# Six gather buffers and six one-hot buffers, in two steps of three groups, in the graph convolutions of a three-layer graph network

## The chip, the cores and the metric

The kernel runs on one core of one Trainium2 chip. The metric is the device time of one execution in microseconds (us). The engines are TensorE (PE for matmuls, PEld for loading weights), VectorE (DVE), ScalarE (ACT), GpSimd (POOL) and the synchronising engine SyncE (SP). SP, ACT and POOL also issue transfers; their queues are written SPq, ACTq and POOLq.

## What is computed

12500 nodes with 96 features, 400000 edges sorted by destination. A first layer passes messages with edge attributes; it is not touched here. Two graph convolutions follow, and with them this change:

```python
def _gcn_conv(x, edge_index, edge_weight, W, b):
    h = x @ W
    row = concatenate([edge_index[0], loop]); col = concatenate([edge_index[1], loop])
    w = concatenate([edge_weight, ones])
    deg = segment_sum(w, col); dinv = where(deg > 0, rsqrt(deg), 0)
    norm = dinv[row] * w * dinv[col]
    return segment_sum(norm[:, None] * h[row], col) + b
for W, b, Wr, br in layers:            # two layers
    h_in = x
    xc = _gcn_conv(x, edge_index, edge_weight, W, b)
    g = sigmoid(h_in @ Wr + br)
    x = relu((1.0 - g) * h_in + g * xc)
```

## The kernel before

After the edge layer, two convolution layers run (l = 0, 1), each over all edges in one pass. In each, the edges go two ways.

The 1736 "main" tiles of 128 edges make 217 groups of 8 tiles. For a group, POOL issues 8 indirect transfers (line 927), each gathering 128 rows of the scaled node table, into one of three row buffers `conv_g[b]`, b = g mod 3; VectorE writes weighted one-hot matrices of the destinations inside a window of 64 nodes into one of two buffers `conv_s[h]`, h = g mod 2, with two operations (`spread_group`, lines 1826 and 1830); TensorE multiplies the 8 tiles into one PSUM bank `sg[h]` (`segment`, line 1123, 16 matmul records for 8 matmuls in float32); VectorE adds the 64 columns to the accumulator `acc` at a start that it reads from a table (`add_group`, line 1841).

The 1400 "side" tiles go through dense adjacency blocks written by the edge layer. 35 units of 40 tiles are each 14 pieces; ACT loads a piece of 980 KB into one of seven ring slots (`load_piece`, line 1352) once the piece seven earlier has been eaten; TensorE multiplies its 7 blocks (`piece`, line 1137, 14 records); after the 14th piece ACT copies the sums to `side_out` (line 1368) and VectorE adds 40 short column ranges to `acc` (`add_side`, line 1854), in four parts of ten.

The two ways are interleaved by hand. TensorE first does the lead, 7 groups, and then per unit 14 pieces with a segment after pieces 1, 3, 6, 8, 10 and 13 (`SEGMENT_AFTER`), 6 groups a unit. In the first 28 units, "mix" work for one half chunk of nodes is done too: TensorE's gate product (line 1145) after the first segment and its own product (line 1149) after the third, VectorE's seven operations (lines 1861 to 1876) after the fourth side part. SP loads the two inputs of that mix (lines 736 and 737) and stores its results (lines 740 and 741).

What orders the work are counting semaphores: `seg` (segments done), `acc` (sums added), `weighted` (one-hots ready), `eaten` (pieces), `out` (side sums copied), `added` (side ranges added). Before the change:

- POOL gathers group n once `seg` shows group n-3; the ids come in steps of three groups, loaded by SP (`load_step`, three transfers, two buffers) once `seg` shows the last group of two steps earlier.
- VectorE spreads group n once `seg` shows n-2, then waits for segment n-1 and adds it, then does a side part.
- TensorE's segment n waits for its rows, for `weighted` of n and for `acc` of n-2.
- SP's order in a unit: wait for the mix of the unit before, load the mix inputs; wait for `seg`, load a step; wait for `added`, load the bases of the side ranges; wait for the mix, store it; wait for the unit's last `seg`, load a step.

## Time and profile before

| | us |
|---|---|
| median of 3 runs | 11193.3 |
| lowest, highest | 11172.85, 11203.12 |
| the profiled execution's own time | 11224.96 |
| its span from first to last instruction | 11223.1 |
| mean granted TensorE clock | 0.85 of 2.4 GHz |

The convolutions take the second half: the first gather of layer 0 is issued at 5693.7 us, layer 0's last piece ends at 8354 us, layer 1 gathers from 8460.5 us and ends its pieces at 11133 us. In a row of the page, "idle before" is the time the engine sat idle just before such instructions, and the name behind the arrow is what ended most of it. "issue" means that no releaser shows; "remote" means that a semaphore update from elsewhere ended the wait. A mean of line 1137 or 1123 counts overlapping halves of one float32 matmul, so the spacing of the starts, not the mean, is the pace.

### The profile page before, as it was taken

Reading aid. Unit: us, or ns where it says so; the run is one execution under the profiler, and the core shown is the slowest. Engines: PE = TensorE matmul, PEld = TensorE weight load, DVE = VectorE, ACT = ScalarE, POOL = GpSimd, SP = SyncE. Lnnn points to the kernel's source line nnn. Section 1 sums busy time; section 2 is a strip of 40 time slices with the busy share of each in tenths; the row PEclk is TensorE's granted clock in tenths of the full one; section 3 lists DMA queues with packets and bytes.
Section 4 is the critical chain, followed back from the end, with each engine's and each line's share of the span. In section 5 each row is a group of like instructions: output and inputs, shape, how many; then the busy total and the mean of one; then the engine's idle time right before and its main releaser. Section 6 shows DMA issues by size and latency. Waiting matters only on the chain. (4 is left out here: it accounts for less than half of the span.)

```text
span 11223.1 us, 161106 instructions
## 1 busy us (share of the span) xinstructions
PE 8285.4 (74%) x40104; PEld 5619.5 (50%) x40104; DVE 5185.2 (46%) x17514; ACT 2896.1 (26%) x6502; POOL 6745.8 (60%) x6696
## 2 busy tenths in 40 slices
PE   5567667676666667766758888888876888888886
PEld 4334444444444444444445655556554555555554
DVE  5566666666666666666622222222222222222223
ACT  4345555555555555555400000000000000000000
POOL 4665555565655565666456666666655666666663
PEclk7688888888888888888768998888887888888887
DMA  4345555565655566666447767677665676766666
GB/s 152 81 130 169 169 170 168 171 174 168 173 167 172 168 173 171 171 172 173 136 147 234 239 228 233 228 235 240 222 201 181 229 235 228 236 233 228 233 225 200
DMA packets 1329031, 2149.86 MB, mean 192 GB/s; under 512 B 306427, under 2 KB 1079948, under 8 KB 1328700
## 3 DMA queue, kind: packets, MB, share of 16 engines
q10 hardware_dynamic: 142400, 986.64, 24.7%
q1 hardware_dynamic: 925996, 684.95, 20.8%
q0 software_dynamic: 260560, 477.49, 15.9%
q14 instruction: 55, 0.45, 0.0%
q8 instruction: 20, 0.33, 0.0%
HBM read 1587.45 MB, written 560.99 MB: 191 GB/s over the span
## 5 line engine op out<-in xcount | busy, mean ns | idle before, releaser
L927 POOL DMA_INDIRECT hid<-conv_table,hid x3452 | 3389.3, 982 | 1962.6 <-issue 1031.5
L883 POOL DMA_INDIRECT hid<-src_table,src_ids x3127 | 3174.7, 1015 | 2115.5 <-ACT msg L1255 1127.1
L1137 PE MATMUL bd<-ring,table_sb 128*96 128x280 f32 x13720 | 3618.3, 421 | 307.3 <-issue 245.0
L1137 PEld LDWEIGHTS bd<-ring,table_sb 128*96 128x96 f32 x13720 | 2341.8, 173 | 1501.4 <-issue 647.2
L1033 PE MATMUL bd<-one_hot_dst,one_hot_src 128*128 128x343 bf16 x8400 | 1753.8, 353 | 1463.7 <-ACT blocks L1263 1193.1
L1033 PEld LDWEIGHTS bd<-one_hot_dst,one_hot_src 128*128 128x128 bf16 x8400 | 840.9, 108 | 2270.9 <-issue 1811.0
L1263 ACT ACTIVATE blocks<-bd 128x686 f32<-128x686 f32 x1400 | 1116.9, 798 | 2289.4 <-remote 1503.7
L1841 DVE TENSOR_TENSOR acc<-acc,sg 96x64 f32 x434 | 94.7, 218 | 2956.3 <-remote 1568.4
L1123 PE MATMUL sg<-conv_hot,hid 128*96 128x64 f32 x6944 | 774.9, 258 | 618.4 <-issue 466.1
L1123 PEld LDWEIGHTS sg<-conv_hot,hid 128*96 128x96 f32 x6944 | 746.1, 176 | 707.7 <-issue 622.5
L1368 ACT ACTIVATE side_out<-bd,side_flag 96x280 f32<-96x280 f32 x70 | 34.3, 490 | 4015.9 <-PE bd L1137 2436.3
L1255 ACT ACTIVATE msg<-hid,msg 128x96 f32<-128x96 f32 x3136 | 905.4, 362 | 153.7 <-DVE msg L1565 124.5
L1052 PEld LDWEIGHTS sg<-hot,msg 128*98 128x98 f32 x6272 | 780.3, 200 | 328.1 <-issue 154.8
L1052 PE MATMUL sg<-hot,msg 128*98 128x64 f32 x6272 | 818.5, 284 | 158.7 <-ACT msg L1255 129.5
L1854 DVE TENSOR_TENSOR acc<-acc,side_out 96x7 f32 x2800 | 462.5, 165 | 947.8 <-issue 620.2
L1585 DVE TENSOR_SCALAR one_hot_src<-one_hot_src,side_now 128x128 bf16<-128x128 bf16 x4200 | 809.4, 259 | 0.0
L1022 PE MATMUL pa<-w_attr,attr 128*128 128x384 f32 x1568 | 677.1, 561 | 62.1 <-DMA attr<-in_attr 36.0
L1022 PE MATMUL pb<-w_attr,attr 128*128 128x384 f32 x1568 | 674.0, 558 | 47.8 <-issue 36.0
L1565 DVE TENSOR_SCALAR msg<-gate_t 128x4 f32<-128x4 f32 x784 | 152.0, 194 | 1196.5 <-ACT gate_t L1248 1008.2
L1242 ACT ACTIVATE hid<-hid 128x768 f32<-128x768 f32 x784 | 654.1, 834 | 195.5 <-issue 104.7
L1582 DVE TENSOR_SCALAR one_hot_dst<-iota_z,side_now 128x688 bf16<-128x688 f16 x1400 | 563.5, 402 | 0.0
L1541 DVE TENSOR_TENSOR hid<-pb,hid 128x768 f32<-128x768 f32 x392 | 373.4, 952 | 293.6 <-DMA hid<-src_table,src_ids 209.6
(208 smaller groups left out, 5412.3 us busy)
## 6 DMA issues: line engine op xcount, KB each, us to landing
ring<-adjacency ACTq DMA_DIRECT2D x980, 980.0 KB
adjacency<-blocks SPq DMA_DIRECT2D x700, 686.0 KB
hid<-conv_table,hid POOLq DMA_INDIRECT x3452
attr<-in_attr SPq DMA_DIRECT2D x392, 128.0 KB
hid<-src_table,src_ids POOLq DMA_INDIRECT x3127
conv_table<-table_sb SPq DMA_DIRECT2D x28, 336.0 KB, 4.7
feat_half<-feat_keep SPq DMA_DIRECT2D x56, 168.0 KB
buf_h<-dinv_rows SPq DMA_DIRECT2D x56, 168.0 KB
```

The costliest lines, as they stand in the source:

```text
L883: pool.indirect_dma_start(out=hid[s][:, t, :], out_offset=None, in_=src_rows, in_offset=bass.IndirectOffsetOnAxis(ap=src_ids[s // 2][:, j: ...
L927: pool.indirect_dma_start(out=conv_g[b][:, t, :], out_offset=None, in_=conv_rows[l], in_offset=bass.IndirectOffsetOnAxis(ap=conv_ids[j][:, ...
L1022: last = nc.tensor.matmul(attr_ps[s % 2][:, 512 * h:512 * h + 2 * H2], attr[s // 2][:, P * (s % 2):P * (s % 2 + 1)], w_attr[:, 2 * H2 * h: ...
L1033: op = nc.tensor.matmul(bd[:, 512 * h:512 * h + HALF_Z], y[:, 1 + k, :], z[:, Z_PAD * h:Z_PAD * h + HALF_Z], start=(k == 0), stop=(k == 2))
L1052: op = nc.tensor.matmul(sg[s // 2][0:ACC_ROWS, 0:WINDOW], msg[s % 2][:, t, :], hot[s % 2][:, t, :], start=(s % 2 == 0 and t == 0), stop=(s ...
L1123: op = nc.tensor.matmul(sg[h][0:D, 0:WINDOW], conv_g[b][:, t, :], conv_s[h][:, t, :], start=(t == 0), stop=(t == GROUP - 1))
L1137: op = nc.tensor.matmul(side_ps, table_sb[:, D * k:D * (k + 1)], ring[slot][:, :, QUAD_FANS * b:QUAD_FANS * (b + 1)], start=(k == 0), stop ...
L1242: nc.scalar.activation(flat, flat, ACT.Gelu).then_inc(s_gelu, 1)
L1255: op = nc.scalar.activation(m[:, t, 0:D], hid[s][:, t, 0:D], ACT.Copy, scale=m[:, t, GATE_ROW:GATE_ROW + 1])
L1263: nc.scalar.activation(blocks[h][:, :, FAN * t4:FAN * (t4 + 1)].rearrange("p (h b) d -> p h b d", h=2), bd[:, :].rearrange("p (h z) -> p h ...
L1582: v.tensor_scalar(z[:, :], iota_z[:, :], side_now[:, 4, t:t + 1], None, ALU.is_equal)
L1585: op = v.tensor_scalar(y[:, 1 + k, :], y[:, 0, :], side_now[:, 1 + k, t:t + 1], None, ALU.mult)
```

## The change

Per layer, rows and one-hots get six buffers each, as two steps j = 0, 1 of three slots. The added buffers lie in space that is free in this phase (the tiles that hold `feat_in`, `x_c`, `buf_h`, `buf_b` at other times, and one new tile). POOL gathers group n once `seg` shows n-6. The three sums of a step are columns of one PSUM bank `sg[j]`; VectorE adds them once all three segments of the step are done, and TensorE's first segment of a step waits until the sums of two steps before have been added. VectorE spreads a whole step ahead of the additions, and does side parts behind the second and third slot of each step, the mix at the end of the unit. SP loads ids for step k+2 once the rows of step k have landed, and the other two streams once the one-hots of step k are weighted, both in the first part of the unit; it no longer waits for `seg` at the unit's end, so that the load of the mix inputs stands right behind the store of the mix before. The core of the diff:

```diff
-CONV_SPARED = [min(GROUP - 1, max(0, PAD_TILES - GROUP * b)) for b in range(STEP_GROUPS)]
-SEG_CREDIT, ACC_CREDIT, SIDE_CREDIT = 3, 2, 1
+CONV_SPARED = [min(GROUP - 1, max(0, PAD_TILES - GROUP * b)) for b in range(LEAD_GROUPS)]
+SEG_CREDIT, ACC_CREDIT, SIDE_CREDIT = 2 * STEP_GROUPS, STEP_GROUPS, 1
...
+        rows_of = [[feat_space[0][:, 0:GROUP * D], feat_space[1][:, 0:GROUP * D], rows_own[0]],
+                   [rows_own[1], rows_own[2], rows_more[:, :]]]
+        hots_of = [[hot_own[0][:, :], x_c[0][:, 0:GROUP * WINDOW], x_c[1][:, 0:GROUP * WINDOW]],
+                   [hot_own[1][:, :], buf_h[1][:, 0:GROUP * WINDOW], buf_b[1][:, 0:GROUP * WINDOW]]]
...
-                def load_step(j, k, late, s=cv[l], skip=0):
-                    g = k * STEP_GROUPS - LEAD_SKIP + skip
-                    groups, width = STEP_GROUPS - skip, GROUP * (STEP_GROUPS - skip)
+                def load_ids(j, k, late, skip=0):
                     sp.dma_start(conv_ids[j][:, GROUP * skip:].rearrange("p (g t) -> p g t", t=GROUP),
-                                 io["src"][bass.ds(late * LATE_GROUPS + g, groups), :, :].rearrange("g p t -> p g t")
-                                 ).then_inc(s[f"step{j}"], 16)
+                                 io["src"][bass.ds(late * LATE_GROUPS + group_of(k, skip), STEP_GROUPS - skip), :, :
+                                           ].rearrange("g p t -> p g t")).then_inc(s_conv_ids[j], 16)
+
+                def load_edges(j, k, late, skip=0):
+                    tile0, width = GROUP * group_of(k, skip), GROUP * (STEP_GROUPS - skip)
                     sp.dma_start(conv_rel[j][:, GROUP * skip:],
-                                 rel_keep[:, bass.ds(late * MAIN_TILES + g * GROUP, width)]).then_inc(s[f"step{j}"], 16)
+                                 rel_keep[:, bass.ds(late * MAIN_TILES + tile0, width)]).then_inc(s_conv_edges[j], 16)
                     sp.dma_start(conv_wt[j][:, GROUP * skip:],
-                                 io["weight"][:, bass.ds(late * SIDE_TILES + g * GROUP, width)]).then_inc(s[f"step{j}"], 16)
+                                 io["weight"][:, bass.ds(late * SIDE_TILES + tile0, width)]).then_inc(s_conv_edges[j], 16)
+
+                def load_step_after(j, m, k, n0, late, s=cv[l]):
+
+                    for slot in slots_of(k):
+                        wait_apart(sp, s_rows[j][slot], rows_gathered(m, j, slot))
+                    load_ids(j, k + 2, late)
+                    wait_apart(sp, s["weighted"], n0 + group_of(k, STEP_GROUPS))
+                    load_edges(j, k + 2, late)
...
                     if more:
-                        wait_apart(sp, s["seg"], n0 + u * UNIT_GROUPS + (LEAD_GROUPS + STEP_GROUPS + SEG_CREDIT))
-                        load_step(1, u * 2 + 5, late)
+                        for k in (LEAD_STEPS, LEAD_STEPS + 1):
+                            load_step_after(k % 2, u + k // 2, u * 2 + k, n0, late)
                     wait_apart(sp, s["added"], nu * SIDE + SIDE_CREDIT)
                     load_base(u)
                     if mix:
                         wait_apart(sp, m["done"], h0 + u + 2)
                         store_mix_half(u)
-                    if more:
-                        wait_apart(sp, s["seg"], n0 + u * UNIT_GROUPS + (LEAD_GROUPS + UNIT_GROUPS + SEG_CREDIT))
-                        load_step(0, u * 2 + 6, late)
 
...
-                def gather_group(g, n, slot, j, b, spared, s=cv[l], l=l):
-                    wait_apart(pool, s["seg"], n + (SEG_CREDIT - STEP_GROUPS + 1))
+                def gather_group(n, j, slot, spared, s=cv[l], l=l):
+                    wait_apart(pool, s["seg"], n + (SEG_CREDIT - 2 * STEP_GROUPS + 1))
...
+                def gather_step(k, j, m, n0, c0):
+
+                    wait_apart(pool, s_conv_ids[j], c0 * (16 * STEPS_OF[j]) + m * 16 + 16)
+                    for slot in slots_of(k):
+                        g = group_of(k, slot)
+                        gather_group(n0 + g, j, slot, CONV_SPARED[g] if isinstance(g, int) else 0)
+
+                def conv_unit(u, n0, c0):
+                    for k in (LEAD_STEPS, LEAD_STEPS + 1):
+                        gather_step(u * 2 + k, k % 2, u + k // 2, n0, c0)
 
...
-                def segment(g, n, b, h, j, s=cv[l]):
-                    pe.wait_ge(s[f"gath{b}"], gathered_group(j, b))
-                    pe.wait_ge(s["weighted"], n + 1)
-                    pe.wait_ge(s["acc"], n + (ACC_CREDIT - 1))
+                def segment(k, j, m, slot, n0, s=cv[l]):
+                    if slot == 0 and not (isinstance(k, int) and k < 2):
+                        pe.wait_ge(s["acc"], n0 + group_of(k - 1, ACC_CREDIT))
+                    pe.wait_ge(s_rows[j][slot], rows_gathered(m, j, slot))
+                    pe.wait_ge(s["weighted"], n0 + group_of(k, slot + 1))
                     for t in range(GROUP):
-                        op = nc.tensor.matmul(sg[h][0:D, 0:WINDOW], conv_g[b][:, t, :], conv_s[h][:, t, :],
-                                              start=(t == 0), stop=(t == GROUP - 1))
+                        op = nc.tensor.matmul(sg[j][0:D, WINDOW * slot:WINDOW * (slot + 1)], conv_g[j][slot][:, t, :],
+                                              conv_s[j][slot][:, t, :], start=(t == 0), stop=(t == GROUP - 1))
                     op.then_inc(s["seg"], 1)
 
...
-                def spread_group(g, n, h, j, slot, s=cv[l]):
-
-                    dve.wait_ge(s["seg"], n + (SEG_CREDIT - 1))
+                def spread_group(n, j, slot, s=cv[l]):
+
+                    dve.wait_ge(s["seg"], n + (SEG_CREDIT - 2 * STEP_GROUPS + 1))
                     cols = slice(GROUP * slot, GROUP * (slot + 1))
...
+                def spread_step(k, j, m, slot, n0, c0):
+
+                    if slot == slots_of(k)[0]:
+                        dve.wait_ge(s_conv_edges[j], c0 * (32 * STEPS_OF[j]) + m * 32 + 32)
+                    spread_group(n0 + group_of(k, slot), j, slot)
+
+                def add_group(k, j, slot, n0, late, sides, s=cv[l]):
+
+                    g = group_of(k, slot)
                     start = dve.value_load(base_i[0:1, bass.ds(late * LATE_GROUPS + g, 1)], min_val=0, max_val=NODES)
                     window = acc[0:D, bass.ds(start, WINDOW)]
-                    dve.wait_ge(s["acc"], n + ACC_CREDIT)
+                    dve.wait_ge(s["acc"], n0 + g + ACC_CREDIT)
                     dve.wait_ge(s["added"], sides + SIDE_CREDIT)
-                    dve.wait_ge(s["seg"], n + (1 + SEG_CREDIT))
-                    v.tensor_tensor(window, window, sg[h][0:D, 0:WINDOW], ALU.add).then_inc(s["acc"], 1)
+                    dve.wait_ge(s["seg"], n0 + group_of(k, STEP_GROUPS) + SEG_CREDIT)
+                    v.tensor_tensor(window, window, sg[j][0:D, WINDOW * slot:WINDOW * (slot + 1)],
+                                    ALU.add).then_inc(s["acc"], 1)
 
...
-                def conv_unit(u, n0, u0, h0, k0, late, with_sides, with_mix, s=cv[l]):
+                def conv_unit(u, n0, u0, h0, c0, late, with_sides, with_mix, more):
 
...
-                        spread_group(g0 + at, m0 + at, at % 2, j, slot)
-                        done = ADD_PART * min(ADD_PARTS, max(0, i - 1)) if with_sides else 0
-                        add_group(g0 + (at - 1), m0 + (at - 1), (at - 1) % 2, late, n + (done - past))
-                        if with_sides and 1 <= i <= ADD_PARTS:
-                            add_side(done, done + ADD_PART, nu - 1, m0 + at)
-                        if i == ADD_PARTS and with_mix:
-                            mix(u, h0 + u)
+                    done, past = 0, SIDE if with_sides else 0
+                    for k in (LEAD_STEPS, LEAD_STEPS + 1):
+                        for slot in range(STEP_GROUPS):
+                            if more or k == LEAD_STEPS:
+                                spread_step(u * 2 + (k + 1), (k + 1) % 2, u + (k + 1) // 2, slot, n0, c0)
+                            add_group(u * 2 + (k - 1), (k - 1) % 2, slot, n0, late, n + (done - past))
+                            if with_sides and slot > 0:
+                                add_side(done, done + ADD_PART, nu - 1, n0 + group_of(u * 2 + (k - 1), slot + 1))
...
-                    conv_unit(0, n0, u0, h0, k0, late, False, True)
+                    for k in range(-1, LEAD_STEPS):
+                        for slot in slots_of(k + 1):
+                            spread_step(k + 1, (k + 1) % 2, (k + 1) // 2, slot, n0, c0)
...
-                        conv_unit(u, n0, u0, h0, k0, late, True, True)
-                    with dve.Fori(HALVES, UNITS) as u:
-                        conv_unit(u, n0, u0, h0, k0, late, True, False)
-                    add_group(MAIN_GROUPS - 1, n0 + (MAIN_GROUPS - 1), (MAIN_GROUPS - 1) % 2, late, all0 + (UNITS - 1) * SIDE)
+                        conv_unit(u, n0, u0, h0, c0, late, True, True, True)
+                    with dve.Fori(HALVES, UNITS - 1) as u:
+                        conv_unit(u, n0, u0, h0, c0, late, True, False, True)
+                    conv_unit(UNITS - 1, n0, u0, h0, c0, late, True, False, False)
+                    for slot in range(STEP_GROUPS):
+                        add_group(STEPS - 1, (STEPS - 1) % 2, slot, n0, late, all0 + (UNITS - 1) * SIDE)
```

## Rows read from the trace of the kernel before

**Rows 1.** page of the profile, parts 1 and 5: busy us, share, count; the gathers.

```profile
PE 8285.4 (74%) x40104; PEld 5619.5 (50%) x40104; DVE 5185.2 (46%) x17514; ACT 2896.1 (26%) x6502; POOL 6745.8 (60%) x6696
...
L927 POOL DMA_INDIRECT hid<-conv_table,hid x3452 | 3389.3, 982 | 1962.6 <-issue 1031.5
```

**Rows 2.** windows: length, busy us (records) of PE, PEld, DVE, ACT, POOL; clock, DMA.

```profile
5926.00:7845.00 1919.00, 1616.99 (x7693) 1138.99 (x7692) 517.13 (x1690) 29.02 (x52) 1231.32 (x1251) 0.89 0.70 233
7845.00:8354.00 509.00, 421.91 (x2040) 299.44 (x2040) 109.68 (x404) 3.43 (x7) 313.96 (x323) 0.89 0.64 216
8694.00:10621.00 1927.00, 1632.57 (x7698) 1135.92 (x7696) 519.62 (x1690) 29.14 (x52) 1234.33 (x1253) 0.89 0.70 232
10621.00:11134.00 513.00, 424.25 (x2040) 303.38 (x2041) 109.62 (x404) 3.43 (x7) 309.77 (x320) 0.88 0.63 212
```

**Rows 3.** timeline of PE: start us, duration, line, operation, count, idle before it.

```profile
7667.39 1.49 PE L1123 MATMUL sg<-conv_hot,hid 128*96 128x64 f32 x16
7675.35 1.24 PE L1123 MATMUL sg<-conv_hot,hid 128*96 128x64 f32 x13
7677.63 0.27 PE L1123 MATMUL sg<-conv_hot,hid 128*96 128x64 f32 x1 [1.04 <-issue]
...
7687.50 7.83 PE L1137 MATMUL bd<-ring,table_sb 128*96 128x280 f32 x22 [0.80 <-issue]
```

**Rows 4.** timeline of POOL beside Rows 3; 14 more gathers in the gap.

```profile
7666.15 0.95 POOL L927 DMA_INDIRECT hid<-conv_table,hid  x1 [2.01 <-remote]
...
7686.15 0.95 POOL L927 DMA_INDIRECT hid<-conv_table,hid  x1 [0.30 <-issue]
7690.04 0.95 POOL L927 DMA_INDIRECT hid<-conv_table,hid  x1 [2.94 <-remote]
```

**Rows 5.** windows of line 1137 alone: no gathers beside it, then with gathers.

```profile
8337.00:8354.00 17.00, 15.83 (x68) 10.62 (x66) 1.00 0.02 4
...
7754.00:7771.00 17.00, 11.26 (x42) 6.60 (x42) 0.88 0.51 158
```

**Rows 6.** timelines of PE, DVE and POOL at the start of layer 0.

```profile
5739.01 2.79 PE L1123 MATMUL sg<-conv_hot,hid 128*96 128x64 f32 x16 [7.59 <-DMA hid<-conv_table,hid]
5754.18 2.82 PE L1123 MATMUL sg<-conv_hot,hid 128*96 128x64 f32 x16 [12.38 <-DVE conv_hot L1830]
...
5777.32 0.22 PE L1123 MATMUL sg<-conv_hot,hid 128*96 128x64 f32 x1 [1.30 <-issue]
...
5798.32 0.59 PE L1123 MATMUL sg<-conv_hot,hid 128*96 128x64 f32 x3 [1.13 <-issue]
...
5752.58 0.22 DVE L1841 TENSOR_TENSOR acc<-acc,sg 96x64 f32 x1 [23.64 <-remote]
...
5753.25 0.97 POOL L927 DMA_INDIRECT hid<-conv_table,hid  x1 [5.98 <-remote]
```

**Rows 7.** timeline around the gate product of one unit (SPq: transfers issued by SP).

```profile
7704.24 0.09 SPq L736 DMA_DIRECT2D feat_half<-feat_keep  x1
...
7711.15 0.99 PE L1145 MATMUL bd<-feat_half,conv_w 96*96 96x448 f32 x2 [2.31 <-DMA buf_h<-dinv_rows]
```

**Rows 8.** waits: who for whom, total us, times, longest; PEld by layer, then POOL.

```profile
PEld bd L1145 <- issue: 35.9, 15, 6.4
...
PEld bd L1145 <- issue: 33.3, 15, 6.9
...
POOL hid L927 <- PE sg L1123: 461.6, 138, 7.1
POOL hid L927 <- remote: 433.3, 183, 6.1
```

**Rows 9.** timeline at the end of layer 0: last sum, then the side columns.

```profile
8355.73 0.22 DVE L1841 TENSOR_TENSOR acc<-acc,sg 96x64 f32 x1 [10.76 <-PE sg L1123]
...
8357.44 2.81 DVE L1854 TENSOR_TENSOR acc<-acc,side_out 96x7 f32 x10 [1.50 <-issue]
...
8375.58 1.09 DVE L1939 TENSOR_TENSOR t_c<-acc,buf_h 96x896 f32<-96x896 f32 x1
```

110 lines of the change are left out of this document (49 added, 61 removed).

## The prediction, made before the changed kernel was run

> **What bounds the kernel now.** Read the windows of the convolution first [rows 2]. The ScalarE counts give the units: a mix unit has two ScalarE records (52 are 26 units), a later one has one. So a mix unit takes 1919/26 = 73.8 us and 1927/26 = 74.1 us in layers 0 and 1, a unit without mix 509/7 = 72.7 and 513/7 = 73.3. No engine is full: PE's busy share there is 84% and its clock 0.89.
>
> Then read what TensorE's instructions cost undisturbed. From one segment to the next, over a segment and two pieces, 7.96 us pass (7667.39 to 7675.35) [rows 3]. A unit is six segments and 14 pieces; two pieces are that less the segment's share, which I put at 1.3 (an estimate), so 6.6 us, so a unit is 7 x 6.6 + 6 x 1.3 = 54 us, plus 2 for the mix products. 16 to 18 us of each unit are lost.
>
> The timelines of TensorE and GpSimd beside each other show where. From 7666.15 POOL runs 16 gathers, two groups, without a rest (start to start 1.25 to 1.6 us) [rows 4]. Ten microseconds into that run TensorE falls from a record every 0.1 us to one every 1.4 to 2.1, inside a segment, where nothing is waited for, and stays so to 7687.50, just as the run ends [rows 3]. The first 17 us after a layer's gathers are done have 68 records of line 1137 at clock 1.00; 17 us inside a unit with gathers have 42 [rows 5]. At the layer's start it is grosser: a segment under way at 5777.3 creeps to 5798.3 [rows 6]. Semaphore updates suffer as well: a segment issued from 5739.01 to 5741.8 is added by VectorE only at 5752.58, and POOL, idle for 5.98 us, resumes at 5753.25, on the same update [rows 6]. I don't know the mechanism; I take from the rows that long runs of gathers slow TensorE, and that rests of POOL end it.
>
> This makes a loop. TensorE alone needs 54/6 = 9 us a group; POOL's gathers need 8 x (3389.3 + 1031.5)/3452 = 10.2 us a group without rests [rows 1], and with 895/434 = 2.1 us of waiting for segments [rows 8] 12.3, which is 73.8/6. TensorE gains on POOL, several segments' updates come at once, POOL runs two groups in a row, TensorE is stalled, POOL catches up and rests. Neither engine alone sets the pace: TensorE's speed is given back in stalls.
>
> **The change, part by part.** Six row buffers instead of three. POOL's condition moves from segment n-3 to n-6. In the steady state POOL is at its limit in either kernel: it waits for the newest segment. A limit three groups further away shifts the loop; it doesn't shorten it. I take 0 for the steady state. From both sides: if a quarter of POOL's 895 us of waiting [rows 8] went, -224; if runs got longer, the price under the third rival.
>
> The start of a layer. POOL's rest of 6 us at 5747.3 goes, since six groups are free at once; TensorE's segment that waited for a one-hot at 5754.18, which itself waited for that update [rows 6], comes some 5 us earlier. Against it, POOL now has three more groups (30.6 us) to gather in one run, in which TensorE, in its first unit, is stalled; before, that first stall took 5777 to 5798, 21 us [rows 6]. I take 16 us more stall, less 6 for the rest and 5 for the earlier segment: +5 a layer, from -11 (no longer stall) to +20 (all 31 us of it).
>
> The end of a layer. POOL is done six segments before TensorE instead of three. Three groups more run at 9 instead of 12.3 us: -10 a layer, 0 if TensorE is behind by then.
>
> Sums added a step at a time. Same three sums, same operations per unit. Two more stand behind the last segment of a layer, ahead of the side ranges, on the path to line 1939. A sum with the register work behind it is 1.71 us (8355.73 to 8357.44) [rows 9]: +3.4 a layer. In the loop nothing waits for them: TensorE needs the bank two steps on, about 30 us later. The last side part moves from behind the fourth segment to behind the third segment's two more sums, two spreads and two side parts, by the count of operations some 2 us later behind the third than before. The copy on ScalarE is due at the unit's end, some 30 us behind the third segment; cover enough, and gone only if a stall of 12 us or more falls on it.
>
> Spreads a step ahead. 12 operations a unit as before; TensorE waited for a one-hot hardly at all, so 0.
>
> SP's queue. The step loads leave the unit's end; the wait for them stood ahead of the mix load. In the unit shown, the load is issued at 7704.24 and TensorE, idle for 2.31 us, starts the gate product when it lands [rows 7]. Now it is issued right behind the mix's store, some 10 us before the unit ends, and the wait goes. TensorE's queue was idle 35.9 + 33.3 = 69 us ahead of line 1145, in 53 of 56 mix units [rows 8], so 73 us in all, 1.3 a unit; next late is nothing. But does a microsecond saved on TensorE shorten a unit? The windows answer: a mix unit has 2 us of products and 1.3 us of this wait more than a unit without, 3.3 us, and is longer by only 1.1 and 0.8 [rows 2]. 0.95/3.3 = 0.29 comes through, -21 us of the 73. With it, six waits on landed rows and two on one-hots a unit replace two on segments in SP's queue; behind them stand only loads that are due later, 0. The ids of a step are loaded when the rows two steps before have landed, 30 us before POOL's need; 0.
>
> Sum over two layers: 2 x 5 - 2 x 10 + 2 x 3.4 - 21 = -24 us. The profiled execution took 11224.96, so 11201; that execution stands 31.7 above the median of the three runs, and the median becomes 11193.3 - 24 = 11169 us.
>
> **The rivals.** First, the mix wait comes through in full: -73 instead of -21, median 11117. For it: it is TensorE's own idle time. Against it: the mix units' lengths [rows 2], though seven units are few beside stalls of ten microseconds.
>
> Second, deeper buffers do free POOL. If TensorE doesn't keep POOL at its limit, the rests go, and a unit comes nearer to POOL's 61 us. With a quarter of the waiting gone: -24 - 224, median 10945. For it: POOL waits for segments 321 times [rows 8]. Against it: the rests seem to be what lets TensorE run. The Trainium skill (Trainium Kernel Development and Optimization, Best Practices) advises double buffering so that transfers overlap compute; read on to more depth, it is on this rival's side. No row here shows a gain from depth.
>
> Third, slower. With six buffers POOL can fall behind its limit by more groups, and then gathers three or four in a run. Each further group in a run stalls TensorE for 10.2 us, in which it does a sixth of its work: 8.5 us. There are about 3452/32 = 108 cycles of four groups; if one in eight gets one more group in its run, that is +115, median 11284. It decides against the old kernel from three such runs on, and to over 0.3% from seven. For it: the start of the layer, where the longest run goes with the longest stall [rows 6]. Against it: updates of more than two segments at once need TensorE ahead by more than a run's length.
>
> Fourth, the change doesn't do what it says: POOL, kept by ids that SP loads late behind its new waits, stays three groups ahead. Then only the mix wait moves: 11193.3 - 21 + 7 = 11179.
>
> **How the numbers follow.** Forecast 0.46 (11115 to 11220), first rival 0.13, second 0.13, third 0.20, fourth 0.08. About 0.3%, 34 us, is what a measurement of this kernel can tell from no change. Of the forecast 0.10 is faster than that, 0.34 within, 0.02 slower; the first two rivals are faster; the third slower; the fourth within, but for 0.01. Together: faster 0.37, within 0.41, slower 0.22. The range leaves out the stronger half of the second and of the third rival: 11010 to 11290.
>
> **What would show it.** Right: mix units of about 73.5 us; no idle time at line 1145; POOL still waiting for segments about 2 us a group; stalls of about ten microseconds as often as before; the stall in a layer's first unit longer by half; the last 50 us of a layer at full pace. Wrong: a unit below 71 us, or POOL's waits gone without new stalls (second rival); stalls of 20 us inside the loop (third); gathers beginning behind a load of ids (fourth). The step most likely to fail is the one that calls the steady state unchanged.

## The result and the profile after

| | before | changed |
|---|---|---|
| median, us | 11203.1 (9 runs) | 11270.7 (9 runs) |
| lowest to highest, us | 11172.9 to 11238.9 | 11244.6 to 11303.0 |
| profiled execution, us | 11224.96 | 11244.56 |

The change makes the kernel slower: ratio 1.0063, 95% interval 1.0044 to 1.0081, or 67.5 us by the medians. The forecast was 24 us faster.

The two profiled executions differ by only 19.6 us, since the changed kernel's is the fastest of its nine. The windows of the changed kernel say where the time went. For each layer they run from the first gather to the second side copy, over the 26 mix units after it, over the seven units without mix, and over what follows. Columns as in [rows 2].

```profile
5653.62:5932.25 278.63, 149.42 (x703) 108.81 (x704) 49.01 (x116) 1.75 (x3) 176.72 (x182) 0.70 0.48 147
5932.25:7853.53 1921.28, 1603.09 (x7697) 1141.30 (x7696) 526.55 (x1690) 29.14 (x53) 1212.32 (x1248) 0.89 0.69 232
7853.53:8350.69 497.16, 414.83 (x2037) 299.94 (x2036) 107.51 (x398) 3.44 (x8) 285.59 (x296) 0.89 0.64 218
8350.69:8453.91 103.22, 50.70 (x211) 47.30 (x209) 51.45 (x103) 13.80 (x15) 24.94 (x15) 0.52 0.70 223
8453.91:8730.77 276.86, 152.11 (x703) 109.60 (x703) 48.93 (x116) 1.75 (x3) 175.89 (x182) 0.70 0.47 144
8730.77:10649.75 1918.98, 1611.38 (x7695) 1138.59 (x7695) 523.98 (x1690) 29.15 (x53) 1199.18 (x1244) 0.89 0.69 233
10649.75:11152.06 502.31, 418.87 (x2040) 297.07 (x2039) 107.25 (x398) 3.43 (x8) 288.95 (x301) 0.89 0.64 216
11152.06:11242.57 90.51, 20.73 (x113) 16.51 (x111) 49.42 (x99) 0.49 (x1) 0.00 (x0) 0.52 0.72 213
```

The same windows of the kernel before:

```profile
5693.68:5925.88 232.20, 145.51 (x699) 107.48 (x699) 44.12 (x111) 1.75 (x3) 150.15 (x153) 0.74 0.50 159
5925.88:7845.37 1919.49, 1617.48 (x7699) 1139.48 (x7697) 517.13 (x1690) 29.14 (x52) 1231.79 (x1252) 0.89 0.70 233
7845.37:8354.38 509.01, 421.92 (x2040) 299.38 (x2039) 109.68 (x404) 3.43 (x7) 313.59 (x323) 0.89 0.64 215
8354.38:8460.53 106.15, 50.70 (x211) 47.28 (x209) 51.43 (x103) 13.79 (x15) 24.97 (x14) 0.51 0.73 237
8460.53:8693.49 232.96, 144.19 (x699) 107.04 (x699) 44.24 (x111) 1.75 (x3) 149.19 (x154) 0.74 0.50 157
8693.49:10620.34 1926.85, 1632.43 (x7699) 1135.92 (x7698) 519.62 (x1690) 29.14 (x53) 1234.72 (x1253) 0.89 0.70 232
10620.34:11133.34 513.00, 424.23 (x2040) 303.22 (x2039) 109.62 (x404) 3.43 (x8) 309.89 (x321) 0.88 0.64 212
11133.34:11223.05 89.71, 20.74 (x113) 16.52 (x111) 48.99 (x97) 0.49 (x1) 0.00 (x0) 0.53 0.72 215
```

Take the differences of the lengths. The starts are longer by 46.4 and 43.9 us. The mix units differ by +1.8 and -7.9, the units without mix by -11.9 and -10.7, the rest by -2.9 and +0.8. That makes +59.6 us from the first gather on, near the 67.5 of the medians. The edge layer ahead of it, which the change doesn't touch, was 40.1 us shorter in this execution (first gather at 5653.6 instead of 5693.7), so the spans differ by 19.5.

The loss therefore lies at the starts. Here is the start of layer 0 after the change. First GpSimd (start, duration, engine, line, operation, idle before it):

```profile
5665.84 1.04 POOL L953 DMA_INDIRECT hid<-conv_table,hid  x1 [11.17 <-DMA hid<-in_src]
...
5751.84 0.94 POOL L953 DMA_INDIRECT rows_more<-conv_table,hid  x1 [0.30 <-issue]
5763.50 1.46 POOL L953 DMA_INDIRECT feat_in<-conv_table,hid  x1 [10.71 <-remote]
```

TensorE in the same stretch:

```profile
5704.10 2.81 PE L1146 MATMUL sg<-conv_hot,feat_in 128*96 128x64 f32 x16 [7.35 <-DMA feat_in<-conv_table,hid]
...
5722.03 0.26 PE L1146 MATMUL sg<-x_c,feat_in 128*96 128x64 f32 x1 [3.23 <-issue]
...
5762.63 1.40 PE L1146 MATMUL sg<-x_c,hid 128*96 128x64 f32 x8 [1.83 <-issue]
5763.83 8.14 PE L1159 MATMUL bd<-ring,table_sb 128*96 128x280 f32 x28
```

And VectorE:

```profile
5737.45 0.69 DVE L1849 TENSOR_TENSOR buf_b<-iota_now,hid 128x512 f32<-128x512 f32 x1 [29.77 <-remote]
...
5762.73 0.69 DVE L1849 TENSOR_TENSOR conv_hot<-iota_now,hid 128x512 f32<-128x512 f32 x1 [20.15 <-remote]
```

With six buffers GpSimd gathers 69 times without a rest, 87 us. The segment issued from 5704.1 to 5706.9 is the one that its next group needs, but GpSimd resumes only at 5763.5, 10.7 us after its last gather. The next two segments take from 5714.4 to 5764.0. From 5716.4 to 5762.6 they crawl, with one record each 2 to 3.5 us and no wait. VectorE sits 29.8 and 20.2 us behind updates that don't come: the first is that of the segment issued from 5693.94 to 5696.8, some 40 us late, the second that of the segment from 5704.1. Before, two runs of 37 and 32 gathers stood there with a rest of six microseconds between them, and one segment crawled for some 21 us [rows 6].

In this text a stall is a stretch of over 1.3 us in which register, wait, branch and transfer-issue instructions take 0.64 to 0.76 us each, or TensorE's weight loads stand 1.25 to 3 us apart with no wait between them; stretches less than 1.5 us apart count as one. Counted so over the trace, the large stalls at the start of layer 0 are 38.5 and 26.6 us in place of one of 21.8, and in layer 1 36.4 and 25.2 in place of 22.4. (The first counts from 5723.4 on; shorter stretches stand ahead of it, from 5697.5.) In the units the stalls grew from 13.1 and 13.6 us to 17.0 and 16.1 a unit, while the wait for the mix inputs went. Such a count can be off by one or two microseconds a unit, depending on how the stretches are joined. Who waits in 5800 to 8330 us, after the change (total us, times, longest):

```profile
POOL hid L953 <- PE sg L1146: 145.9, 37, 5.6
POOL hid L953 <- remote: 111.0, 51, 5.7
...
PEld bd L1167 <- issue: 0.5, 1, 0.5
```

Against 35.9 us ahead of the gate product in layer 0 before [rows 8], 0.5 is left. In this unit the load is issued 26 us ahead of its product, not 7 us as in [rows 7] (SP's queue, then TensorE):

```profile
6507.96 0.31 SPq L764 DMA_DIRECT2D feat_half<-feat_keep  x1
...
6533.93 0.94 PE L1167 MATMUL bd<-feat_half,conv_w 96*96 96x448 f32 x2
```

At the end of layer 0 the last three sums stand 1.03 us apart, where [rows 9] shows one:

```profile
8352.03 0.22 DVE L1871 TENSOR_TENSOR acc<-acc,sg 96x64 f32 x1 [15.11 <-PE sg L1146]
8353.06 0.22 DVE L1871 TENSOR_TENSOR acc<-acc,sg 96x64 f32 x1 [0.80 <-DVE acc L1871]
8354.09 0.22 DVE L1871 TENSOR_TENSOR acc<-acc,sg 96x64 f32 x1 [0.82 <-DVE acc L1871]
```

### The profile page after: what moved, and what is told of

Same layout as the page of the kernel before. It is cut to its first block, busy times and chain, and to the rows that moved or that the text cites. A ratio compares the mean times of both kernels' runs of the same rounds, so it can differ in the third digit from the quotient of the medians.

```text
span 11242.6 us, 161615 instructions
## 1 busy us (share of the span) xinstructions
PE 8235.0 (73%) x40104; PEld 5614.5 (50%) x40104; DVE 5197.6 (46%) x17514; ACT 2896.6 (26%) x6502; POOL 6709.2 (60%) x6696
## 3 DMA queue, kind: packets, MB, share of 16 engines
q0 software_dynamic: 260560, 477.49, 15.9%
## 4 chain that ended last, share of the span: by engine, by line
PE 56%; issue 15%; another core or an unknown queue 15%; ACT 7%; DVE 3%; DMA 2%; POOL 1%; DVEq 1%; ACTq 1%; SPq 0%; POOLq 0%
PE bd L1159 30%; PE bd L1055 11%; PE sg L1146 6%; ACT blocks L1286 3%; PE pb L1044 3%; PE sg L1074 2%; PE pa L1044 2%; ACT hid L1265 2%; ACT msg L1278 1%; ACT gate_t L1271 1%; PE bd L1108 1%; PE bd L1171 0%; PE bd L1167 0%; DMA out_nodes<-s_c 0%
## 5 line engine op out<-in xcount | busy, mean ns | idle before, releaser
L1159 PE MATMUL bd<-ring,table_sb 128*96 128x280 f32 x13720 | 3580.3, 420 | 254.6 <-issue 145.1
L953 POOL DMA_INDIRECT hid<-conv_table,hid x1724 | 1660.3, 963 | 1058.5 <-issue 512.4
L953 POOL DMA_INDIRECT feat_in<-conv_table,hid x1152 | 1121.3, 973 | 618.3 <-issue 334.0
L953 POOL DMA_INDIRECT rows_more<-conv_table,hid x576 | 557.0, 967 | 328.5 <-issue 168.4
```

What stands on the lines that cost most here:

```text
L953: pool.indirect_dma_start(out=conv_g[j][slot][:, t, :], out_offset=None, in_=conv_rows[l], in_offset=bass.IndirectOffsetOnAxis(ap=conv_ids ...
L1159: op = nc.tensor.matmul(side_ps, table_sb[:, D * k:D * (k + 1)], ring[slot][:, :, QUAD_FANS * b:QUAD_FANS * (b + 1)], start=(k == 0), stop ...
```

## The experiments

The kernels of a group ran on one chip beside the kernel before; ratios are to that. The groups ran on different chips. The theory is called filling: GpSimd has to gather three groups more than before in one unbroken run, TensorE and VectorE crawl through it, and this costs the 67 us. The first rival is that the change costs in every unit.

**Three groups ahead, with all else changed.**

```diff
-                    wait_apart(pool, s["seg"], n + (SEG_CREDIT - 2 * STEP_GROUPS + 1))
+                    wait_apart(pool, s["seg"], n + (SEG_CREDIT - STEP_GROUPS + 1))
```

> The changed kernel with one number put back: GpSimd gathers group n once segment n-3 is done, through the whole of both layers, though six row buffers are there. Theory S (start): the change lost its time where a layer starts. There GpSimd now gathers 70 rows' worth of transfers in one run instead of 37, and TensorE crawls for 38.5 and 26.6 us in the profile instead of 21.8; from the first gather to the first copy of the side sums 199.6 and 201.8 us pass instead of 166.1 and 165.5, and the second unit is 13 and 8 us longer. Held to three groups, the start is the old one: about 45 us a layer come back, 11270 - 90 = 11180 us, ratio 0.998 to before. Rival T (throughout): the loss is spread over the units (the step-wise additions, the queue order, more stalls), and the start was only where GpSimd's lead was built up: the time stays above 11240.

Measured: 11519.7 against 11518.2 us, ratio 1.0002, interval 0.9989 to 1.0016; 0.998 was expected. (This chip is 2.8% slower with the kernel before, too.) The loss is gone with this one number, so over the whole kernel the step-wise sums, the spreads ahead and SP's order together cost and gain nothing that can be measured. Its windows at the starts, first gather to second side copy:

```profile
5911.15:6160.42 249.27, 147.17 (x694) 107.29 (x695) 49.07 (x116) 1.75 (x4) 154.03 (x158) 0.73 0.49 156
...
8718.60:8966.80 248.20, 147.62 (x700) 107.42 (x701) 49.10 (x116) 1.75 (x3) 153.46 (x158) 0.73 0.50 155
```

**Three groups ahead in the lead and the first unit, six later.** GpSimd's first unit is taken out of its loop and waits as in the diff above; the rest stays as changed.

> The changed kernel with GpSimd held to three groups ahead in the lead and in the first unit alone, and six from the second unit on. Theory S in its plain form (the first unit is a bad place for a long run): the start is the old one, the end keeps what six groups give, 11160 to 11180 us. Theory F (filling): the three extra groups have to be gathered in one long run at some time, and TensorE crawls through that run wherever it stands; then the loss only moves to the second unit, and the time is between 11220 and 11270.

Measured: 11587.4 us, ratio 1.0060 (1.0040 to 1.0079). The loss is back in full.

```profile
5919.90:6197.25 277.35, 151.53 (x700) 108.11 (x701) 49.04 (x116) 1.75 (x3) 173.85 (x180) 0.69 0.47 148
...
8753.68:9030.14 276.46, 150.52 (x699) 108.40 (x699) 49.02 (x116) 1.75 (x3) 172.25 (x178) 0.70 0.47 146
```

The stretch to the second side copy is 28 us longer than in the kernel held throughout, and as long as in the changed kernel on the first chip (278.6 and 276.9), though GpSimd was set free 13 groups later. TensorE, behind it, was still in its first unit (207.7 us from the first gather to the first side copy). The fill can be seen in layer 0. GpSimd gathers 48 times without a rest, and TensorE, at full pace until 6076, gives one record each 1.4 to 2.9 us until 6125.7, a stall of 51.4 us (GpSimd, then TensorE):

```profile
6057.57 0.97 POOL L953 DMA_INDIRECT hid<-conv_table,hid  x1 [2.52 <-remote]
...
6129.64 1.03 POOL L953 DMA_INDIRECT hid<-conv_table,hid  x1 [11.21 <-PE sg L1147]
...
6070.53 5.38 PE L1160 MATMUL bd<-ring,table_sb 128*96 128x280 f32 x22
...
6121.49 0.62 PE L1160 MATMUL bd<-ring,table_sb 128*96 128x280 f32 x1 [2.17 <-issue]
```

So the fill costs as much there as at the very start; a fill in a later unit comes below. These two kernels differ in the depth alone, and by this pair the depth accounts for 28 of the 44 to 46 us that a start grew. The kernel held throughout starts no faster than the kernel before: 249.3 and 248.2 us against 240.5 and 233.8 of the next kernel on this chip, which is the kernel before but for one load. Whether the other parts of the change cost these 9 and 14 us, or it is chance in single profiles, isn't shown.

**The mix load moved early, in the kernel before.**

```diff
                         store_mix_half(u)
+                    if ahead:
+                        load_mix_half(u + 1)
```

> The kernel before with one part of the change: the load of a unit's mix inputs is issued right behind the store of the mix before, ahead of the wait for the unit's last segment. Theory L (loop): TensorE no longer waits at the gate product (35.9 + 33.3 us in the profile of before go to under 5), but what it gains it gives back in stalls: 11203 within 0.15%, units of 73.8 us. Rival W: the wait was on the path, the whole of it comes through: 73 us less, 11130. The forecast stood between, at 21 us less, 11182.

Measured: 11529.9 us, ratio 1.0015 (1.0003 to 1.0027). TensorE's queue waits

```profile
PEld bd L1147 <- issue: 16.7, 16, 1.9
```

ahead of the gate product in both layers together, instead of 69 (under 5 was expected). Not one microsecond of it reaches the time. In this profile a mix unit takes 75.1 and 75.6 us and has 15.4 and 16.7 us of stalls. The part of the forecast that gave 21 us for this is refuted, and so is the full 73.

**Rests for GpSimd.** To test whether unbroken runs cause the stalls, a small fill with a wait for it stands before the segment wait and before the fifth gather of each group:

```diff
+                    def rest(t):
+                        at = [0, 4]
+                        if t in at:
+                            r = at.index(t)
+                            idle = (buf_h, buf_b)[r % 2][1][0:1, 512:896]
+                            pool.memset(idle, 0.0).then_inc(s_idle[l], 1)
+                            wait_apart(pool, s_idle[l], n * 2 + (r + 1))
```

> The changed kernel with two rests of GpSimd in each group of eight gathers: a fill of 384 elements in a spare place (about 0.4 us by the fills in the profile, about 0.6 with its wait) before the group's wait for a segment, and another after the fourth gather. Theory R (runs): TensorE crawls because gathers follow each other unbroken for more than ten microseconds; with a rest each five microseconds the stalls go, GpSimd needs 61.5 + 12 x 0.6 = 69 us a unit and sets the pace: 70 x 5 us less than 11270, so 10900 to 10950. Rival N (number): what slows TensorE is that so many gathers are under way, breaks of half a microsecond change nothing: units stay at 73.8 or grow by up to 7 us, 11270 to 11700.

Measured: 11482.0 us, ratio 0.9970 (0.9958 to 0.9982), against 1.0063 for the changed kernel on its chip. The stalls went from 16.5 to 0.7 and 0.8 us a unit. TensorE's timeline inside a unit has no single records any more; it waits for gathered rows instead:

```profile
7000.65 6.80 PE L1172 MATMUL bd<-ring,table_sb 128*96 128x280 f32 x28
7010.42 1.63 PE L1159 MATMUL sg<-x_c,feat_in 128*96 128x64 f32 x16 [2.97 <-DMA feat_in<-conv_table,hid]
7011.84 11.76 PE L1172 MATMUL bd<-ring,table_sb 128*96 128x280 f32 x42
7025.15 1.57 PE L1159 MATMUL sg<-x_c,hid 128*96 128x64 f32 x16 [1.54 <-DMA hid<-conv_table,hid]
```

The mechanism is borne out, and the size was missed (10900 to 10950 us was expected). GpSimd issues its 48 gathers a unit in 74.0 us here and in 73.9 in the changed kernel, so their mean rate is the same; what the rests change is that no run is longer than four. A rest costs not 0.6 but 1.0 us: from the end of one gather to the start of the next 1.38 us pass in the rows below, 1.22 at the other rest of a group, and 0.30 without one. Twelve of them on 61.5 give the 74.0 us a unit takes, now at GpSimd's pace. The stalls were given up for rests of about the same length:

```profile
7008.33 0.41 POOL L956 MEMSET buf_h<- 1x384 f32 x1
7009.71 0.95 POOL L966 DMA_INDIRECT hid<-conv_table,hid  x1 [0.97 <-POOL buf_h L956]
```

**One rest a group, shorter rests, rests in the kernel before, and narrow gathers, on chips without stalls.** The next two groups ran on two other chips. The edits are `at = [0]`; fills of 8 elements; the same rests on the kernel before; and gathers of 24 of the 96 columns.

> The changed kernel with one rest of GpSimd in each group of eight gathers, a fill of 384 elements ahead of the wait for the segment; the run with two rests a group showed that such a rest takes 1.0 us (from 0.30 to 1.27 us between two gathers), that the stalls went from 16.5 to 0.8 us a unit, and that GpSimd then set the pace with 61.5 + 13 = 74 us. Theory R: a run of eight gathers, 10 us, is still short enough for updates to get through; the stalls stay away and a unit is 61.5 + 6.5 = 68 us, 400 us less than with two rests a group, ratio 0.963 to before. Rival D: a rest must come each five microseconds; runs of ten microseconds let the stalls back in by ten or so microseconds a unit, and the ratio is 0.99 to 1.00.

> The changed kernel with two rests a group as before, but fills of 8 elements instead of 384, some 0.3 us shorter each. Theory R: what helps is that the run is broken, also by 0.7 us; stalls stay near 1 us a unit, and a unit is 61.5 + 12 x 0.7 = 70 us, ratio 0.997 - 70 x 4/11500 = 0.973. Rival D: the rest has to last a microsecond, so that the updates that wait get through; the stalls come back, ratio 0.985 to 1.00.

> The kernel before (three row buffers) with one rest a group as in the run on the changed kernel, fills of 384 elements. Theory R: GpSimd paused there in any case once it had caught up; the rest costs nothing, breaks the runs of 16 and takes the stalls away, ratio 0.965 to 0.98. Rival B (buffers): with three row buffers GpSimd can't be a group ahead any more and waits for the segment on top of its rest; the ratio is 0.99 or more, and the six buffers are what makes rests pay.

> The changed kernel with each gather fetching 24 instead of 96 columns of a row (from another place of the table), the other 72 columns of the row buffers filled with zero once: as many gathers and descriptors, a quarter of the bytes; the convolution's result is left out. Theory R (GpSimd's issuing is what crowds out TensorE's instructions, not the rows that are moved): gathers still start 1.25 us apart, the stalls are there as in the changed kernel, 13 to 17 us a unit, ratio 1.00 to 1.01. Rival M (memory traffic): with a quarter of the bytes the stalls go or halve, and the ratio is 0.98 or below.

> The changed kernel itself beside the kernel before, on one chip with the three that follow. The last four ran on a chip on which the kernel before takes 9173 us and TensorE is never stalled (0 stalls found in four kernels, where the two chips used earlier had 13 to 17 us of them a unit); there GpSimd, unbroken at 61.5 us a unit, set the pace. Theory F (filling): where the chip has the stalls, the ratio is 1.005 to 1.008, from the start of the layers alone; where it has none, a longer run of gathers costs nothing, GpSimd is never held, and six buffers are worth what little TensorE still held it up: 0.995 to 1.000. Rival T (the change costs in every unit): 1.005 or more on both.

> The changed kernel with one rest of a microsecond in each group, again, wanted on a chip that has the stalls. There theory R says: stalls gone, units of 68 us as on the chip without them, ratio 0.965 to 0.975. Rival D (a rest is needed each five microseconds): stalls of ten or so microseconds a unit stay, 0.99 to 1.00. On a chip without stalls both say 1.05, as measured.

> The kernel before with one rest a group, again. On a chip with the stalls, theory R: 0.965 to 0.98, as the kernel with six buffers but for 0.2%; rival B (three buffers don't leave room for a rest): 0.99 or more. On a chip without stalls 1.054, as measured.

> The changed kernel with gathers of a quarter of the bytes, again (the convolution's result is left out). On a chip with the stalls, theory R (GpSimd's issuing crowds out the instructions, not the rows moved): 13 to 17 us of stalls a unit, ratio 1.00 to 1.01. Rival M (memory traffic): the stalls halve or go, ratio 0.97 or below. On a chip without stalls 1.0035, as measured.

Measured, with the kernel before at 9172.7 us (first four) and 9211.4 us (last four). Of the first four expectations, written for a chip with stalls, three missed; the fourth (1.00 to 1.01) holds in its ratio, but not in the stalls that it names:

| | us | ratio (interval) |
|---|---|---|
| one rest a group | 9651.5; 9689.9 | 1.0518 (1.0500 to 1.0536); 1.0516 |
| two short rests a group | 9789.9 | 1.0675 (1.0657 to 1.0693) |
| one rest, kernel before | 9671.9; 9697.0 | 1.0543 (1.0525 to 1.0560); 1.0519 |
| narrow gathers | 9201.7; 9229.6 | 1.0035 (1.0021 to 1.0048); 1.0020 |
| the changed kernel | 9228.5 | 1.0015 (1.0006 to 1.0025) |

The kernel before takes 18% less time here, and next to no stall is found in any of the profiles. Part 4 of the changed kernel's page on such a chip, the chain that ended last:

```profile
POOL 50%; issue 29%; DMA 8%; PE 8%; DVE 2%; ACT 1%; POOLq 1%; DVEq 1%; SPq 0%; ACTq 0%
```

Its windows from the first gather to the second side copy, and over the 26 mix units:

```profile
4554.20:4751.63 197.43, 136.86 (x699) 102.10 (x700) 47.55 (x114) 1.75 (x4) 142.21 (x146) 0.79 0.62 198
4751.63:6363.32 1611.69, 1515.68 (x7699) 1084.90 (x7698) 524.46 (x1690) 29.14 (x53) 1230.56 (x1250) 0.97 0.83 277
```

A mix unit is 62.0 us, GpSimd's 48 gathers at 1.25 us and little else, and the start is 80 us shorter. But for one gather at its start, GpSimd issues a layer's 1725 in one run, with 0.3 us between two of them. The change costs 0.15% here. That misses the expectation (0.995 to 1.000 by the theory, 1.005 or more by the rival), but lies on the theory's side: without stalls even the longest run is almost free. It also shows that more depth gains nothing even where GpSimd alone sets the pace. What these runs can't tell is what the stalls hang on.

**The same questions on a chip with stalls.** The kernel before took 11504.8 us beside the next four. In the last one ScalarE loads two of ten quads of a piece.

> The changed kernel with two rests of a microsecond a group in the lead and the first unit of each layer alone (13 groups), and none later. If the chip has the stalls, theory F (the loss is the stall in the long run that fills six buffers): with two rests a group throughout, 157 us passed from a layer's first gather to its first side copy and 75 for the next unit, against 200 and 77 in the changed kernel; the start alone gives that back, 2 x 45 us, ratio 1.006 - 0.008 = 0.998, and the later units keep their 16 us of stalls. Rival: the lead of six groups itself costs (rows that wait, updates that come later); the ratio stays at 1.004 or more. On a chip without stalls, both: 1.0015 + 26 rests of 1 us in two layers, 1.007.

Measured: 11565.9 us, ratio 1.0056 (1.0039 to 1.0072); the expectation, 0.998, was wrong. Layer 0 reaches its first side copy 156.5 us after the first gather, as expected, but then takes 128.3 us for one unit:

```profile
5930.07:6214.93 284.86, 149.69 (x704) 109.64 (x704) 49.19 (x118) 1.75 (x4) 186.38 (x206) 0.70 0.46 142
...
8760.81:9045.67 284.86, 149.53 (x703) 109.17 (x704) 49.00 (x116) 1.75 (x4) 186.75 (x206) 0.72 0.46 141
```

With rests GpSimd is the slower side and builds no lead; when they end, it fills the six buffers in one run of 52 gathers, from 6078.8 to 6144.0 us, and stalls of 29.0 and 30.4 us stand from 6089.5 to 6152.3, in TensorE's second unit. (In layer 1 the run is one of 44 gathers and comes earlier: 189.1 us to the first side copy, 95.8 for the next unit.) The fill was put off, not avoided, and cost as much there. The ratio is what the expectation's rival named, that the lead of six groups itself costs. The windows speak against it: once the lead is there, a mix unit takes 74.5 and 74.4 us, against 74.5 and 75.0 in the kernel held to three groups, and the excess lies in the unit with the long run. A lead that is built up without a long run was not tried on a chip with stalls.

> The changed kernel with one rest of a microsecond in each group, for a chip that has the stalls. Theory R: a run of eight gathers is short enough; the stalls go and a unit takes 68 us as on the chip without them, ratio 0.965 to 0.975. Rival D: runs of ten microseconds let ten or so microseconds of stall a unit back in, 0.99 to 1.00. On a chip without stalls 1.052, as twice measured.

Measured: 11490.9 us, ratio 0.9993 (0.9982 to 1.0005), with 13.7 and 13.5 us of stalls a unit. Rival D was right: with runs of eight gathers most of the stalls stay. One rest a group is too little:

```profile
7012.62 0.75 PE L1172 MATMUL bd<-ring,table_sb 128*96 128x280 f32 x1 [0.67 <-issue]
7014.05 0.62 PE L1172 MATMUL bd<-ring,table_sb 128*96 128x280 f32 x1 [0.68 <-issue]
7016.16 0.63 PE L1172 MATMUL bd<-ring,table_sb 128*96 128x280 f32 x1 [1.49 <-issue]
```

> The changed kernel with gathers of a quarter of the bytes (the convolution's result is left out), for a chip that has the stalls. Theory R (GpSimd's issuing is what slows the other engines, not the rows that are moved): 13 to 17 us of stalls a unit, ratio 1.00 to 1.01. Rival M (memory traffic of the gathers): the stalls halve or go, ratio 0.97 or below. On a chip without stalls 1.002 to 1.0035, as measured.

Measured: 11569.3 us (two runs), ratio 1.0061 (1.0041 to 1.0081), 16.7 and 18.6 us of stalls a unit. The bytes gathered have no part in it that shows:

```profile
7124.22 0.22 PE L1151 MATMUL sg<-buf_h,hid 128*96 128x64 f32 x1 [1.85 <-issue]
7126.33 0.27 PE L1151 MATMUL sg<-buf_h,hid 128*96 128x64 f32 x1 [1.90 <-issue]
```

> The changed kernel with ScalarE's ring loads cut to two of ten quads from the eighth piece on (a fifth of the bytes and packets; the side part of the convolution is left out by it, the multiplications are all there). For a chip that has the stalls, theory R: TensorE's instructions are slowed by gathers alone, stalls stay at 13 to 17 us a unit, ratio 1.00 to 1.01. Rival Q (the queues of the transfers are full: it takes ring loads and gathers together): without the ring's 980 KB a piece the stalls go, units near 62 us, ratio 0.93 or below. On a chip without stalls 1.00.

Measured: 11563.6 us (two runs), ratio 1.0056 (1.0036 to 1.0076), 16.9 and 17.5 us of stalls a unit. The last column of its windows falls from 232 to 79 GB/s and the units stay as long:

```profile
6208.32:8152.59 1944.27, 1610.85 (x7704) 1135.75 (x7702) 526.95 (x1690) 29.14 (x52) 1214.34 (x1251) 0.89 0.33 79
```

So the bytes moved aren't the cause either. What is left, of what was varied, is GpSimd's own issuing of gathers without a rest. The gathers' transfers themselves are not ruled out: their queue has 260560 packets in every one of these kernels, narrow gathers included.

**Two short rests a group, changed kernel and kernel before.**

> The changed kernel with two rests a group of 0.7 us each (fills of 8 elements), for a chip that has the stalls. Two rests of a microsecond took the stalls from 16.5 to 0.8 us a unit, and GpSimd then paced the unit with 74 us; one rest a group left 13.6 us of stalls. Theory R in the form that is left (a run of four gathers, five microseconds, is short enough, whatever the rest lasts): stalls near 1 us, GpSimd's 61.5 + 12 x 0.7 = 70 us set the pace, 70 x 4 us less than with the longer rests, ratio 0.972. Rival D (what counts is the share of time in which GpSimd is silent, 13 us a unit): with 9 us of rests, stalls of four or more microseconds a unit come back and take the gain, 0.99 to 1.00. On a chip without stalls 1.0675, as measured.

> The kernel before, with three buffers, and the same two short rests a group. Theory R: with rests GpSimd sets the pace and never gets six groups ahead, so three buffers do as well: within 0.3% of the changed kernel with these rests, about 0.973. Rival B: with three buffers GpSimd waits for a segment behind its rests, 0.98 to 1.00.

Measured, again on a chip without stalls (kernel before 9174.7 us): 9780.7 us, ratio 1.0654 (1.0634 to 1.0673), and 9799.0 us, 1.0676 (1.0653 to 1.0699). Six buffers and three agree within 0.3% under rests. Whether short rests end the stalls stays open.

## Why the prediction was wrong

**The bound, and the loop.** Right in what it used: on such a chip stalls that follow GpSimd's runs slow the units. Rests end them, and fewer bytes don't. One reading was off. The rest at 5747.3 ended, and VectorE's sum at 5752.58 came, on the update of this segment, the fourth of the layer (GpSimd had gathered six groups, and the seventh waits for the fourth segment), not of the one issued from 5739.01:

```profile
5728.62 2.80 PE L1123 MATMUL sg<-conv_hot,hid 128*96 128x64 f32 x16 [7.18 <-DMA hid<-conv_table,hid]
```

So the kernel before already held an update back for 21 us, not 11, in its longest run of gathers: the warning was stronger than I read it.

**Six row buffers in the steady state: 0.** Right. GpSimd is at its new limit as before: its waits for segments come to 950 us in 434 groups, 2.2 us a group, against 2.1. No run of gathers in the mix units is longer than 16; among the seven units after them, layer 0 has one of 23. The mix units moved by +1.8 and -7.9 us over 26.

**The start of a layer: +5, from -11 to +20.** This is the step that failed, in size and in one sign. Measured were +46.4 and +43.9. I priced the three extra groups as 16 us more stall and booked the rest that goes as 6 us gained, and the earlier segment as 5. But that rest stood between two runs and let TensorE recover. Without it the runs of 37 and 32 became one of 69 and one of 32, and the large stalls of layer 0 rose from 21.8 to 65.1 us (38.5 + 26.6), 43 more. That this is nearly the 46 by which the start grew is in part chance: all stalls up to the second side copy rose from 37.4 to 106.0 us, 69 more, and not each of them adds its length. In an experiment that changes the depth alone, the price is 28 us a start. My own account of the loop said that rests of GpSimd end the stalls, and I used it for the units and not for the start. The upper bound, all 31 us of the extra gathers, was none, since it supposed that the old run stayed as it was.

**The end of a layer: -10.** Right: the seven units without mix lost 11.9 and 10.7 us, and between the kernel held throughout and the one set free later 15.9 us in layer 0 (518.9 against 503.0). GpSimd's last gather is 46.9 us ahead of the last side copy, not 17.9.

**Sums of a step: +3.4.** Too much: a sum costs 1.03 us, so 2.1 for two, and what follows the last side copy moved by -2.9 and +0.8 us. Three sums in a row cost less than three with other work between them.

**The mix wait: -21.** The wait went, as forecast; its 29% share of gain didn't come. I took it from the difference between mix units and seven others, whose noise I had named. The early load alone gave +0.15%, not -0.19%. A microsecond given to TensorE inside this loop seems to come back as stall: of the changed kernel's 3.9 and 2.5 us more stall a unit, 1.3 would be this.

**The sum.** With the measured starts (+90) and ends (-23), the mix wait at nothing and the sums as forecast (+7), the forecast's own sum gives 74, near the 67.5 of the medians.

**The rivals.** The first fell with the mix wait. The third had the mechanism, more groups in a run stall TensorE for longer, but put it into the units, where it comes about once, in layer 0's last ones, and not into the start, where it was certain. The second fell: the mix units are 73.9 and 73.8 us long. The Trainium skill's advice on double buffering (Trainium Kernel Development and Optimization, Best Practices), read on to more depth, isn't borne out here: with stalls the mix units of the two layers take 74.5 and 75.0 us held to three groups, 75.0 and 74.6 free to six, and without stalls six buffers are 0.15% slower over the whole kernel. The fourth fell: 69 gathers in one run need the six buffers.

**What stays open.** Why a rest of a microsecond each five microseconds suffices and one each ten doesn't. Why TensorE endures the first 50 us of the long run, while it mostly waits for rows, and falls 10 us into a run inside a unit. Which way the gathers slow the other engines. Two ways can be left out by the traces: the gathers' transfers aren't queued up (the last of them has moved by 5754, the core's DMA engines are idle until 5760, and TensorE crawls on), and no code is being loaded (the queues that load instructions move nothing in layer 0's 26 mix units). The Trainium skill (NOTIFIC — the notification-queue block, 7.1 Overflow: three behaviours, one of which stalls the engine) says that the block that writes the engines' trace records holds its producers back inside rather than lose a record. That would suit engines which all take 0.7 us an instruction, but no run here shows it.

## What to carry to other kernels

A deeper buffer must first be filled, and the fill is one long burst of the producer: look in the trace at what the others do in the longest burst that is already there, and price the whole new burst, with the rest between bursts that it swallows. Where two engines hold each other in a loop, a wait taken from one of them is worth nothing until an experiment shows otherwise; take away one wait alone and see. Ask before tuning against a stall whether every chip has it: two rests of a microsecond a group gain 0.3% on one chip, and one such rest, or two short ones, cost 5 to 7% on another.

## What the hardware showed that was not expected

The kernel before took 11203, 11518 and 11505 us on three chips, and 9173, 9211 and 9175 us on three others, nearly all runs within 0.4% of these medians. In the convolutions the difference is the stalls: 13 to 17 us a unit on the first, none on the others, with the same gather pace of 1.25 us. More than half of it lies elsewhere: the edge layer ahead of the first gather takes 5653.6 us in one profile of the changed kernel and 4554.2 in the other, and what slows it wasn't examined. During a stall TensorE, VectorE and SP all take some 0.7 us for an instruction that needs no wait, updates of semaphores arrive up to 56 us late (a segment done at 5706.9, GpSimd going on at 5763.5), and neither gathering a quarter of the bytes nor cutting the total traffic to a third ends it. A stall also outlasts a long run: GpSimd's 69 gathers ended at 5752.8 and TensorE crawled on to 5762.6. The mean granted clock of TensorE, which is either at 2.4 GHz or at half of it, is 0.89 in the units with stalls and 0.97 in those without.
